# Dense rows of a graph network: four layer products made from x one by one, or from one input by folded weights

## The chip, the core and the metric

The kernel runs on one core of a Trainium2 chip. The metric is the device time of one execution in microseconds. Three runs took 3486.61, 3483.99 and 3440.52 us; the median is 3483.99.

## The reference, cut to what matters

There are 50,000 rows of 128 floats and 12,500 edges sorted by their target. Everything is f32.

```
h = relu(layernorm(x))
x = x + leaky(  (h + neighbours(h)) @ W0.T + b0, 0.01 )
h = relu(layernorm(x))
for l in range(4):                    # GAT layer, with a self loop for each row
    h = h @ W[l]
    h = segment_sum(h[src] * softmax_over_edges_of_dst(...), dst) + b[l]
    h = (h - mean(h)) * rsqrt(var(h) + 1e-5) * gamma[l] + beta[l]
x = x + h
```

A row that is no edge's target has only its self loop, whose softmax weight is 1. For such a row a layer is a product with W[l], a bias, and a normalisation. The kernel computes all 50,000 rows as if they were like that (the dense rows) and writes them out; the rows with edges are computed apart, and their results overwrite the others at the end.

## The kernel before, in words

The weights are centred once in setup (`WC`, L364), so that a product with them has mean zero over its 128 outputs and only the sum of squares is left to find for a normalisation. Gamma and beta of layer l are applied while the turned rows of layer l + 1 are copied out of PSUM (L697).

`dense` (L568) works on groups of 500 rows, four tiles of 125 rows. It is called five times. The first call has `SHARES[0] * DS` = 40 groups and runs beside the 350 gathers and scatters that GpSimd issues for the edges (`first_moves`, L976). The other four calls have 15 groups each, one call before each attention layer, and run beside 100 gathers of edge rows (`refresh`, L1196). All work of a call is one block: every engine meets the others at its end (L615).

A group makes five visits, `k` = 0 to 4, in each of which its rows are normalised (into `Y`), turned by four transposes (L210), copied to `XT` with a relu or with gamma and beta (L695, L697), and multiplied by four products of 128 columns (L221) after a bias product (L217). Visit 0 is the convolution with `W0`, visits 1 to 4 are the layers. In visits 1 to 3 ScalarE squares 512 elements per partition (L680), VectorE sums them (L735), ScalarE takes the root (L202), VectorE inverts it (L759) and multiplies the product by it (L777). After visit 4 the squares are summed by ScalarE itself (L676), and VectorE multiplies by gamma (L787) and adds to the row (`finish`, L795). GpSimd adds beta of the last layer to the row beforehand (L628).

Visits are ordered in rounds (`in_rounds`, L556): five groups make visit 0, then the same five visit 1, and so on. Each engine walks through the visits in its own written order, with fixed offsets between its steps, and waits on semaphores. Rows lie in a ring of ten groups; SP stores a finished group (L159, L160), and loads another into its place one group later. GpSimd spreads its gathers over the whole list of visits.

Around it: `setup` (L277 to L415), the edge terms (L484 to L551), the two convolution stages for the edges (L1003 to L1193), and `attention` (L1210), which uses `XT`, `Y` and all eight banks in a way of its own. The last attention stage ends with 100 scatters into the output (L232).

In setup VectorE makes its steps one after the other: centring, attention vectors, bias rows split into three bf16 parts (L378 to L382), then the masks of the edges. SP waits for the bias parts (L294), stores them as rows of `BR` (L296), fills a table in memory, and then loads the edge attributes.

## Time and profile before

| | us |
|---|---|
| median of three runs | 3483.99 |
| the profiled execution | 3488.22 |
| its span, first to last instruction | 3486.5 |
| the five dense stages | 1693.5 |
| TensorE busy | 2234.9 |
| VectorE busy | 2147.7 |
| ScalarE busy | 1723.3 |
| GpSimd busy | 1377.2 |
| mean granted TensorE clock, share of 2.4 GHz | 0.677 |

A matmul's busy time is that of overlapping instructions taken together, and its mean is that of one instruction from start to end, so the mean times the count is more than the busy time. A product of four tiles shows as eight matmuls, since one f32 tile takes two passes; a transpose shows as one. Engines: PE is TensorE, PEld its weight loads, DVE VectorE, ACT ScalarE, POOL GpSimd, SP the engine that only issues transfers.

### The profile page before, as it was taken

The numbers are of one execution on the slowest core, as the hardware profiler recorded it, in microseconds if no ns is written. First come the engines' busy times: TensorE is split into PE (matmuls) and PEld (weight loads), VectorE is DVE, ScalarE is ACT, GpSimd is POOL, SyncE is SP. The second block draws the span as 40 slices with busy tenths as digits, with TensorE's granted clock in tenths as the row PEclk, the third lists the DMA queues.
The fourth block names the chain that finished last, engine by engine and source line by source line (L and its number), as shares of the span: only waits on it lengthen the run. The fifth ranks groups of instructions, "written<-read, shape, count | busy, mean of one in ns | idle before, by whom it ended". The sixth has DMA issues, their size and how long they took to land. (4 is left out here: it accounts for less than half of the span.)

```text
span 3486.5 us, 45031 instructions
## 1 busy us (share of the span) xinstructions
PE 2234.9 (64%) x11717; PEld 1789.5 (51%) x11717; DVE 2147.7 (62%) x8249; ACT 1723.3 (49%) x5173; POOL 1377.2 (40%) x1089
## 2 busy tenths in 40 slices
PE   2788888886546488890288891188894088797000
PEld 2666666664334366780166781166683066686000
DVE  2367776666888567448767448777446867412880
ACT  0265665554557556444566444566445456422340
POOL 5588778670112466000366000266100076200367
PEclk9976775565555566995567895566697566678555
DMA  6221222110002311000311000311000311003011
GB/s 123 59 50 32 45 67 55 31 19 15 0 0 79 102 34 26 16 1 0 107 34 26 16 1 0 106 34 26 17 1 1 96 26 42 18 1 71 3 31 37
DMA packets 101670, 126.29 MB, mean 36 GB/s; under 512 B 59443, under 2 KB 67563, under 8 KB 98091
## 3 DMA queue, kind: packets, MB, share of 16 engines
q1 hardware_dynamic: 38634, 97.42, 9.8%
q0 software_dynamic: 62400, 25.68, 4.4%
q8 instruction: 90, 1.47, 0.2%
q14 instruction: 114, 0.93, 0.1%
q10 hardware_dynamic: 432, 0.79, 0.1%
HBM read 78.68 MB, written 64.50 MB: 41 GB/s over the span
## 5 line engine op out<-in xcount | busy, mean ns | idle before, releaser
L227 POOL DMA_INDIRECT S<-row_t,INFG x400 | 516.5, 1291 | 1101.1 <-issue 1101.1
L221 PE MATMUL bank<-WC,XT 128*125 128x128 f32 x4800 | 845.9, 330 | 0.0
L221 PEld LDWEIGHTS bank<-WC,XT 128*125 128x125 f32 x4800 | 712.6, 227 | 172.7 <-issue 172.7
L210 PE MATMUL bank<-ident,Y 125*128 125x125 f32 x2200 | 443.7, 354 | 434.1 <-ACT Y L708 396.3
L210 PEld LDWEIGHTS bank<-ident,Y 125*128 125x128 f32 x2200 | 355.0, 189 | 481.1 <-issue 394.1
L217 PE MATMUL bank<-BR,ones 3*125 3x512 bf16 x725 | 385.1, 531 | 125.9 <-ACT XT L697 75.7
L735 DVE TENSOR_REDUCE ss<-Y 125x4 f32<-125x512 f32 x300 | 205.6, 685 | 367.6 <-ACT Y L680 367.6
L221 PE MATMUL bank<-W,XT 128*125 128x128 f32 x1200 | 310.4, 438 | 44.2 <-ACT XT L1033 44.2
L697 ACT ACTIVATE XT<-bank,BC,GC 128x500 f32<-128x500 f32 x300 | 230.3, 768 | 185.7 <-PE bank L210 185.7
L221 PEld LDWEIGHTS bank<-W,XT 128*125 128x125 f32 x1200 | 265.8, 326 | 108.5 <-issue 54.6
L217 PEld LDWEIGHTS bank<-BR,ones 3*125 3x125 bf16 x725 | 107.1, 148 | 273.8 <-ACT XT L697 118.9
L1256 ACT ACTIVATE XT<-bank,BC,GC 128x500 f32<-128x500 f32 x150 | 114.5, 763 | 268.4 <-PE bank L210 268.2
L1282 DVE COPY SCS<-bank 125x8 f32 (+1 forms) x100 | 16.7, 167 | 357.5 <-PE bank L1236 357.5
L695 ACT ACTIVATE XT<-bank 128x500 f32<-128x500 f32 x200 | 116.8, 584 | 225.5 <-PE bank L210 225.5
L680 ACT ACTIVATE Y<-bank 125x512 f32<-125x512 f32 x300 | 177.5, 592 | 95.1 <-PE bank L221 95.1
L777 DVE TENSOR_TENSOR Y<-bank,rr 125x512 f32<-125x512 f32 x300 | 207.5, 692 | 10.2
L708 ACT ACTIVATE Y<-R,nm,rr 125x128 f32<-125x128 f32 x500 | 211.7, 482 | 0.0
L868 DVE SCALAR_TENSOR_TENSOR R<-R,keep (+1 forms) x496 | 189.9, 414 | 34.9 <-ACT R L1373 30.0
L1236 PE MATMUL bank<-SD,XT 128*125 128x64 f32 x1600 | 205.4, 286 | 0.0
L722 DVE BATCH_NORM_STATS2 st<-R 125x6 f32<-125x128 f32 x800 | 173.3, 279 | 49.4 <-issue 49.4
L1236 PEld LDWEIGHTS bank<-SD,XT 128*125 128x125 f32 x1600 | 202.7, 206 | 0.0
L628 POOL TENSOR_TENSOR R<-R,B 125x512 f32<-125x512 f32 x100 | 131.1, 1311 | 164.8 <-PE bank L210 163.3
(205 smaller groups left out, 3961.8 us busy)
## 6 DMA issues: line engine op xcount, KB each, us to landing
R<-in_x SPq DMA_DIRECT2D x100, 224.0 KB
out_rows<-R SPq DMA_DIRECT2D x100, 224.0 KB
row_t<-T SPq DMA_DIRECT2D x20, 1120.0 KB
S<-row_t,INFG POOLq DMA_INDIRECT x400
R<-in_edge_attr SPq DMA_DIRECT2D x1, 5600.0 KB
x_t<-R SPq DMA_DIRECT2D x5, 1120.0 KB
S<-x_t SPq DMA_DIRECT2D x1, 5600.0 KB
R<-in_x SPq DMA_DIRECT2D x100, 26.0 KB
```

The costliest lines, as they stand in the source:

```text
L210: ins = nc.tensor.transpose(ps[:, a * P:(a + 1) * P], t, ident[0:P, 0:P])
L217: nc.tensor.matmul(pz[0:P, :, :], ones3[:, 0:P], BR[:, bias:bias + 1, :].broadcast_to([3, Q, D]), start=True, stop=False, skip_group_check ...
L221: ins = nc.tensor.matmul(pz[0:P, a, :], xt[:, a * P:(a + 1) * P], w, start=bias is None and a == 0, stop=True, skip_group_check=True)
L227: pool.indirect_dma_start(to, None, table, bass.IndirectOffsetOnAxis(ap=idx, axis=0), bounds_check=rows - 1, oob_is_err=False).then_inc(do ...
L680: nc.scalar.activation(Y[:, s, :, :], DPZ[s][0:P, :, :], ACT.Square, scale=D ** -0.5).then_inc(sq_ready.s, 1)
L697: ins = nc.scalar.activation(XT[:, q % 4, :], DPT[q % 3][:, 0:Q * P], ACT.Identity, bias=BC[:, k - 2:k - 1], scale=GC[:, k - 2:k - 1])
L708: ins = nc.scalar.activation(Y[:, s, a, :], rows(g)[:, a, :], ACT.Identity, bias=nm[:, s, a:a + 1], scale=rr[:, s, a:a + 1])
L722: ins = nc.vector.bn_stats(st[:, q % 2, a, :], rows(g)[:, a, :])
L735: nc.vector.tensor_reduce(ss[:, s, :], Y[:, s, :, :], AX.X, ALU.add).then_inc(var_ready.s, 1)
L777: nc.vector.tensor_tensor(Y[:, s, :, :], DPZ[s][0:P, :, :], wide(rr[:, s, :]), ALU.mult).then_inc(y_ready.s, 1)
L868: return nc.vector.scalar_tensor_tensor(column(R, n, a, 1), column(R, n, a, 0), scalar_of(keep, n, a), column(R, n, a, 1), ALU.mult, ALU.add)
L1236: ins = nc.tensor.matmul(PT[r][0:P, a * D:a * D + SW], XT[:, r, a * P:(a + 1) * P], SD[:, l, :], start=True, stop=True, skip_group_check=True)
```

## The change

Setup multiplies the layers' weights: `AC[:, l]` takes the input of the first layer straight to the output of layer l, for l = 0 to 3, without its normalisations. A normalisation divides a whole row by one number, so the product of the folded weights is right up to that number and up to the biases, which enter with factors that depend on the norms before. `PC` and `KC` hold the products of weights and biases that the norms need. `EB` holds the folded bias rows, one block per tile, placed by 16 transfers of one row each.

A group now makes two normalisations (visit 0 and 1 of before), one convolution, and then, from one turned input: four products with six columns (`DOTS`), four products with 384 columns (`layers`, the first three layers side by side), whose squares ScalarE sums one tile and layer at a time (`norms`), sixteen operations on 125x4 on VectorE with three roots on ScalarE that give the factors of the biases (`sums` to `fourth`), one small transpose of these factors (`turn_s`), four products with 128 columns for the last layer, and one f32 bias product over 13 rows and 512 columns. Then it ends as before: squares, root, gamma, addition.

The order is no longer in rounds: in slot t each engine runs a fixed list of steps, each for the group t minus its lag, with lags up to 7. `SHARES` counts groups, 68 in the first call and 8 in each of the others. GpSimd issues `moves * (t + 1) // groups` gathers by slot t, that is all of them within as many slots as there are groups. Rows lie in a ring of 12. The edge stages take their semaphores from a shared set, which changes no instruction order in them. The diff is cut to its core; further small steps (`statistics`, `aggregate`, `invert`, `scale`, `normalise`, `slope`, `leak`, `join`) do what they did.

```diff
-STEPS = 2 + L - 1
+XS = 12
+KS = 3 * Q + 1
...
-SHARES = [8, 3, 3, 3, 3]
+SHARES = [68, 8, 8, 8, 8]
...
-        DPT, DPZ = banks[0:3], [tiles_of(b) for b in banks[3:8]]
+        HALVES = (0, 1, 1, 0)
+        TURN, CONV, LAYERS, LAST = banks[0], tiles_of(banks[1]), banks[2:4], banks[4:6]
+        DOTS = [b[:, 0:Q * 6].rearrange("p (a n) -> p a n", a=Q) for b in banks[6:8]]
+        TURNS = [b[0:KS, 0:P] for b in LAST]
...
+                sp.wait_ge(s_e4, 1)
+                sp.wait_ge(s_ebz, 1)
+                for a in range(Q):
+                    for j in range(3):
+                        sp.dma_start(EB[j * Q + a:j * Q + a + 1, a * D:(a + 1) * D],
+                                     E4[j + 1:j + 2, :]).then_inc(s_eb, 16)
+                    sp.dma_start(EB[KS - 1:KS, a * D:(a + 1) * D], E4[0:1, :]).then_inc(s_eb, 16)
+                sp.wait_ge(s_eb, 16 * 4 * Q)
...
+                pe.wait_ge(s_cent, 1)
+                for l in range(L):
+                    ins = nc.tensor.matmul(PT[1][:, l:l + 1], brow[:, l, :], ones[0:1, 0:1], start=True, stop=l == 0)
+                    if l:
+                        ins = nc.tensor.matmul(PT[1][:, l:l + 1], WC[:, l, :], BC[:, l - 1:l], start=False, stop=True)
+                ins.then_inc(s_ccol, 1)
+                nc.tensor.transpose(PT[2][:, 0:D], WC[:, 0, :], ident[:, :]).then_inc(s_made, 1)
+                for l in range(1, L):
+                    pe.wait_ge(s_kept, l)
+                    nc.tensor.matmul(PT[2 + l % 2][:, 0:D + l], AC[:, l, :], XE[:, l - 1, 0:D + l], start=True,
+                                     stop=True).then_inc(s_made, 1)
+                pe.wait_ge(s_kept, L)
+                for l in range(1, L):
+                    nc.tensor.transpose(PT[2][:, l * D:(l + 1) * D], XE[:, l, 0:D], ident[:, :])
+                for l in range(1, L):
+                    nc.tensor.matmul(PT[3][:, (0, 1, 3)[l - 1]:(0, 1, 3)[l - 1] + l], XE[:, l - 1, 0:D],
+                                     XE[:, l - 1, D:D + l], start=True, stop=True)
+                nc.tensor.transpose(PT[3][0:L, 128:128 + D], XE[:, L - 1, D:D + L], ident[:, :])
+                pe.wait_ge(s_pairs, 1)
+                nc.tensor.matmul(PT[3][:, 16:26], ones[:, :], GP, start=True, stop=True).then_inc(s_made, 1)
...
+                for l in range(1, L):
+                    ch.add(nc.vector.tensor_scalar(AC[:, l, :], WC[:, l, :], GC[:, l - 1:l], None, ALU.mult))
+                dve.wait_ge(s_ccol, 1)
+                ch.link(nc.vector.tensor_copy(CCOL[:, :], PT[1][:, 0:L]))
+                for l in range(L):
+                    dve.wait_ge(s_made, l + 1)
+                    nc.vector.tensor_copy(XE[:, l, D + l:D + l + 1], CCOL[:, l:l + 1])
+                    nc.vector.tensor_copy(XE[:, l, 0:D + l], PT[2 + l % 2][:, 0:D + l]).then_inc(s_kept, 1)
+                dve.wait_ge(s_kept, L)
...
-                    for q in slots:
-                        upto = moves * max(q, 0) // (max(slots) - 8)
-                        upto = min(upto, moves)
+                    for t in slots:
+                        upto = moves * min(t + 1, groups) // groups
                         move(pool, done, upto)
                         done = upto
-                        if q - 8 in visit and visit[q - 8][1] == 1:
-                            pool.wait_ge(*t_done.at(nth[q - 8]))
-                            xs = rows(visit[q - 8][0])
-                            nc.gpsimd.tensor_tensor(xs, xs, B3[:, :].unsqueeze(1).broadcast_to([P, Q, D]),
+                        if 0 <= t - 3 < groups:
+                            pool.wait_ge(*turned2.at(t - 2))
+                            nc.gpsimd.tensor_tensor(rows(t - 3), rows(t - 3),
+                                                    B3[:, :].unsqueeze(1).broadcast_to([P, Q, D]),
                                                     ALU.add).then_inc(beta_added.s, 1)
...
+                    def turn1(g):
+                        pe.wait_ge(*y1_vector.at(g + 1))
+                        pe.wait_ge(*y1_scalar.at(g + 1))
+                        if g - 2 >= 0:
+                            pe.wait_ge(*copied2.at(min(g - 1, groups)))
+                        transposes(TURN, [Y[:, g % 2, a, :] for a in range(Q)]).then_inc(turned1.s, 1)
...
+                    def turn2(g):
+                        pe.wait_ge(*y2_vector.at(g + 1))
+                        pe.wait_ge(*y2_scalar.at(g + 1))
+                        if g + 1 >= 0:
+                            pe.wait_ge(*copied1.at(min(g + 2, groups)))
+                        transposes(TURN, [Y[:, 2 + g % 2, a, :] for a in range(Q)]).then_inc(turned2.s, 1)
...
+                    def last_layer(g):
+                        pe.wait_ge(*s_copied.at(g + 1))
+                        for a in range(Q):
+                            nc.tensor.matmul(last_of(g)[:, a, :], h0(g, a), AC[:, 3, :], start=a == 0, stop=False,
+                                             skip_group_check=True)
+
+                    def add_biases(g):
+                        nc.tensor.matmul(LAST[g % 2][0:P, :], SB[:, g % 2, :], EB[:, :], start=False,
+                                         stop=True, skip_group_check=True).then_inc(last_done.s, 1)
+
+                    def turn_s(g):
+                        pe.wait_ge(*s3_ready.at(g + 1))
+                        if g >= 2:
+                            pe.wait_ge(*multiplied.at(g - 1))
+                        nc.tensor.transpose(TURNS[g % 2], SV[:, g % NS, :],
+                                            ident[0:P, 0:P]).then_inc(s_turned.s, 1)
+
+                    def layers(a):
+                        def op(g):
+                            if a == 0:
+                                pe.wait_ge(*copied2.at(g + 1))
+                                if g >= 2:
+                                    pe.wait_ge(*mixed2.at(g - 1))
+                                for b in range(Q):
+                                    nc.tensor.matmul(DOTS[g % 2][0:P, b, :], h0(g, b), PC[:, :], start=True,
+                                                     stop=True, skip_group_check=True)
+                            if a == 0 and g or a >= 2:
+                                pe.wait_ge(*normed.at(g * Q + (0, 0, 2, 2)[a]))
+                            nc.tensor.matmul(LAYERS[HALVES[a]][0:P, 0:3 * D], h0(g, a), AC[:, 0:3, :], start=True,
+                                             stop=True).then_inc(layers_done.s, 1)
+                        return op
+
+                    for t in slots:
+                        run(t, [(5, last_layer), (3, layers(3)), (2, turn2), (5, add_biases), (0, turn1),
+                                (2, layers(0)), (2, layers(1)), (0, conv), (4, turn_s), (2, layers(2))])
...
+                    def norms(a):
+                        def op(g):
+                            n = g * Q + a
+                            act.wait_ge(*layers_done.at(n + 1))
+                            if a == 0 and g >= NS:
+                                act.wait_ge(*third_sum.at(g - NS + 1))
+                            for l in range(3):
+                                ins = nc.scalar.activation(JUNK[:, HALVES[a] * 3 + l, :], LAYERS[HALVES[a]][0:P, l * D:(l + 1) * D],
+                                                           ACT.Square, scale=D ** -0.5,
+                                                           accum_out=NRM[:, g % NS, l, a:a + 1])
+                            ins.then_inc(normed.s, 1)
+                        return op
...
+                    def s_root(n, ready, done):
+                        def op(g):
+                            act.wait_ge(*ready.at(g + 1))
+                            nc.scalar.activation(SV[:, g % NS, n * Q:(n + 1) * Q], chain(g)[:, n, :], ACT.Sqrt,
+                                                 bias=KC[0:P, (0, 1, 4)[n]:(0, 1, 4)[n] + 1]).then_inc(done.s, 1)
+                        return op
...
+                    for t in slots:
+                        run(t, [(3, copy2), (6, square_last), (0, root1), (1, copy1), (2, root2),
+                                (5, s_root(2, third_sum, s3_ready)), (6, root_last),
+                                (4, s_root(0, first_sum, s1_ready)), (3, norms(0)), (3, norms(1)), (2, normalise2),
+                                (5, copy_s), (4, s_root(1, second_sum, s2_ready)), (1, slope), (0, normalise1),
+                                (3, norms(2)), (3, norms(3))])
...
+                    def sums(g):
+                        c = chain(g)
+                        dve.wait_ge(*normed.at((g + 1) * Q))
+                        nc.vector.tensor_tensor(c[:, 0, :], NRM[:, g % NS, 0, :], dots(g, 0),
+                                                ALU.add).then_inc(first_sum.s, 1)
+                        nc.vector.tensor_tensor(c[:, 3, :], NRM[:, g % NS, 1, :], dots(g, 1), ALU.add)
+                        nc.vector.tensor_tensor(c[:, 4, :], NRM[:, g % NS, 2, :], dots(g, 3), ALU.add).then_inc(mixed1.s, 1)
+
+                    def with_s1(g):
+                        c = chain(g)
+                        dve.wait_ge(*s1_ready.at(g + 1))
+                        for o, k, n in ((5, 3, 2), (6, 7, 4), (7, 8, 5)):
+                            ins = nc.vector.scalar_tensor_tensor(c[:, o, :], s_of(g, 0), k_of(k), dots(g, n),
+                                                                 ALU.mult, ALU.add)
+                        ins.then_inc(mixed2.s, 1)
...
+                    def finish(g):
+                        dve.wait_ge(*multiplied.at(g + 1))
+                        dve.wait_ge(*beta_added.at(g + 1))
+                        nc.vector.tensor_tensor(rows(g), rows(g), FR[:, g % 2, :, :], ALU.add).then_inc(out_ready.s, 1)
+
+                    for t in slots:
+                        run(t, [(3, normalise2), (0, statistics1), (2, leak), (5, with_s2), (2, join),
+                                (0, aggregate1), (2, statistics2), (5, times_s2), (2, aggregate2), (4, sums),
+                                (5, third), (6, sum_last), (7, multiply), (0, invert1), (6, invert_last),
+                                (2, invert2), (0, scale1), (5, fourth), (4, with_s1), (2, scale2), (4, times_s1),
+                                (0, normalise1), (4, second), (7, finish)])
...
-            dense(done * DS, SHARES[l + 1] * DS, C, refresh, [(s_refresh, 16 * C * (l + 1))])
+            dense(done, SHARES[l + 1], C, refresh, [(s_refresh, 16 * C * (l + 1))])
```

## Rows read from the trace of the kernel before

**Rows 1.** The page: the span, and the granted clock in 40 equal slices, in tenths.
```profile
span 3486.5 us, 45031 instructions
PEclk9976775565555566995567895566697566678555
```
**Rows 2.** Busy time in windows, dense stages: first, second, sum of all five.
```profile
core 0: us, PE busy (x) PEld busy (x) DVE busy (x) ACT busy (x) POOL busy (x), PEclk, DMA share, GB/s
138.80:826.20 687.40, 574.83 (x2600) 441.66 (x2600) 455.51 (x1760) 386.86 (x1120) 495.76 (x390) 0.67 0.20 46
1179.50:1432.90 253.40, 198.00 (x975) 151.50 (x975) 171.50 (x660) 145.09 (x420) 148.95 (x115) 0.69 0.15 37
...
sum 1693.50, PE 1357.02 PEld 1041.24 DVE 1142.40 ACT 967.75 POOL 1091.62; mean PE 271.40 PEld 208.25 DVE 228.48 ACT 193.55 POOL 218.32
```
**Rows 3.** The same view: a round, a slow round, parts of a round, 100 us of attention.
```profile
301.90:380.40 78.50, 65.04 (x324) 50.01 (x324) 56.78 (x217) 47.37 (x139) 62.77 (x52) 0.70 0.19 35
556.40:652.00 95.60, 87.96 (x326) 67.96 (x326) 57.87 (x222) 48.84 (x143) 72.34 (x57) 0.50 0.19 38
302.00:349.00 47.00, 38.19 (x144) 29.29 (x144) 34.75 (x147) 24.82 (x74) 39.46 (x32) 0.50 0.26 57
350.00:380.00 30.00, 25.77 (x178) 20.20 (x177) 21.53 (x68) 21.05 (x65) 22.22 (x20) 1.00 0.08 2
2000.00:2100.00 100.00, 100.00 (x785) 88.43 (x784) 43.69 (x111) 50.30 (x93) 0.00 (x0) 1.00 0.00 1
```
**Rows 4.** Groups by line in the round 301.9 to 380.4 us (busy us, mean ns).
```profile
L697 ACT ACTIVATE XT<-bank,BC,GC 128x500 f32<-128x500 f32 x15 | 11.5, 766 | 8.5 <-PE bank L210 8.5
L777 DVE TENSOR_TENSOR Y<-bank,rr 125x512 f32<-125x512 f32 x15 | 10.4, 692 | 0.5
L735 DVE TENSOR_REDUCE ss<-Y 125x4 f32<-125x512 f32 x15 | 10.3, 686 | 16.4 <-ACT Y L680 16.4
L708 ACT ACTIVATE Y<-R,nm,rr 125x128 f32<-125x128 f32 x24 | 10.2, 482 | 0.0
L680 ACT ACTIVATE Y<-bank 125x512 f32<-125x512 f32 x15 | 8.9, 591 | 4.2 <-PE bank L221 4.2
L759 DVE RECIPROCAL rr<-rt 125x4 f32<-125x4 f32 x24 | 4.0, 168 | 0.1
```
**Rows 5.** Timeline (start, length in us), instructions of one line merged.
```profile
301.99 0.26 ACT L676 ACTIVATE Y<-bank 125x128 f32<-125x128 f32 x1
302.24 0.26 ACT L676 ACTIVATE Y<-bank 125x128 f32<-125x128 f32 x1
307.50 2.07 PE L221 MATMUL bank<-W,XT 128*125 128x128 f32 x8
311.98 1.04 PE L210 MATMUL bank<-ident,Y 125*128 125x125 f32 x4
...
508.22 1.14 PE L221 MATMUL bank<-WC,XT 128*125 128x128 f32 x8
```
**Rows 6.** Timeline: one gather, and the pause before it.
```profile
507.61 1.27 POOL L227 DMA_INDIRECT T<-in_x,dstI  x1 [0.30 <-issue]
```
**Rows 7.** Groups by line on GpSimd, 1180 to 1400 us.
```profile
L227 POOL DMA_INDIRECT S<-row_t,INFG x100 | 129.1, 1291 | 51.1 <-issue 51.1
```
**Rows 8.** Single lines, whole span: min/median/max ns; last, busy us and mean.
```profile
L221 PE MATMUL bank<-WC,XT x4800: 272/273/577, 171.4 to 3197.5; 128*125 128x128 f32 x192
L1236 PE MATMUL bank<-SD,XT x1600: 219/273/417, 1441.7 to 3199.2; 128*125 128x64 f32 x178
L764 DVE SCALAR_TENSOR_TENSOR nm<-mv,rr x200: 149/161/1379, 144.4 to 2976.2; 125x4 f32<-125x4 f32 x100
...
L535 PE MATMUL bank<-VE,XT 128*125 128x4 f32 x200 | 42.3, 336 | 0.0
```
**Rows 9.** Timeline in setup: the last bias part, the three transfers after it.
```profile
25.81 0.48 DVE L382 CAST R<-R 1x640 bf16<-1x640 f32 x1
26.32 1.88 SPq L296 DMA_DIRECT2D BR<-R  x3
```
**Rows 10.** Groups by line on TensorE, 2000 to 2100 us: one of two such rows.
```profile
L210 PE MATMUL bank<-ident,S 125*128 125x125 f32 x76 | 11.2, 269 | 0.0
```

625 lines of the change are left out of this document (351 added, 274 removed).

## The prediction

> **What bounds the kernel now.** Read the page first for the span and for the granted clock of TensorE, which swings between its two levels (1.2 and 2.4 GHz) all through the dense stages [rows 1]. Then cut the span into stages: five dense stages, the first with 40 groups of 500 rows and four with 15 each, take 1693.5 of 3486.5 us, 16.9 us a group; that is all that the change rewrites [rows 2]. Then cut one dense stage into rounds of five groups. A round takes 78.5 us, 15.7 us a group, while VectorE is busy 56.8 of it (11.4 a group), ScalarE 47.4 (9.5) and TensorE 65.0 (13.0). Its first 47 us run at clock 0.50 and the next 30 at 1.00, and one round that never got the high clock took 95.6 us [rows 3]. So the half-clock stretches set the pace, with TensorE as the engine that is late and VectorE next behind. The rows of the two clocks differ by almost two: a product of four tiles is 2.07 or 1.14 us [rows 5]. Every dense stage is a block of its own and all engines meet at its end, so it counts with its whole length.
>
> GpSimd matters in a second way. It issues a gather every 1.57 us [rows 6], and each of the four later dense stages has 100 of them [rows 7]: 157 us below which no such stage can go. Now the stages are 251 to 253 us, so the gathers are covered.
>
> **The change, per group.** VectorE: the three wide reductions and the three wide products by the inverse root go, with three inversions [rows 4]: 3 x (0.686 + 0.692 + 0.168) = 4.64 us. Sixteen operations on 125x4 come instead, the recurrence for the three norms. The same form takes 0.161 in the middle [rows 8], so 2.6 us; the bounds are 0.1 (four small ones overlapped) and 0.24 each, 1.6 to 3.8 us. One more normalising tile comes, taken from ScalarE, 0.3 as I estimate. Busy: 11.4 - 4.6 + 2.6 + 0.3 = 9.7 us, and some 30 pauses of 0.03 between operations make 10.6. That is the floor of a slot.
>
> ScalarE: three wide squares and three scaled copies go, 3 x (0.591 + 0.766) = 4.07, and one normalising tile, 10.2 / 24 = 0.43 [rows 4]; three roots go and three come. Twelve squares of one tile with a sum come. Such squares start 0.25 us apart [rows 5], and for the last read of each batch I add half of that: 12 x 0.25 + 4 x 0.13 = 3.5, and a small copy, 0.3 as for one square. So 9.5 - 4.5 + 3.8 = 8.8, with pauses 9.4 us.
>
> TensorE: one tile's product is two passes, a transpose one. From 2.07 us for eight passes, of which the last takes about 0.42, a pass is 0.236 at the low clock, and from 1.14 and 0.27 it is 0.124 at the high one; a transpose is 0.21 by its 1.04 us for four, and half at the high clock [rows 5]. Transposes fall from 20 to 9. Product columns stay the same: conv and last layer are 8 passes each, and the layers' product is 8 passes of 384 columns. A pass of 64 columns lasts 0.219 where one of 128 lasts 0.272 at best [rows 8], so 128 columns more cost 0.107 at the high clock and 0.213 at the low: 0.34 or 0.66 a pass, 2.7 or 5.3 us (bounds: no dearer than a 128 pass, 1.9 at the low clock; three times it, 5.7). The dots with six columns are 8 passes; the nearest, with four, take 42.3 / 200 = 0.21 each where the weights are as large [rows 8], hardly less than 128 columns do, so 0.95 or 1.9. The bias product in f32 has 512 columns twice: 0.9 or 1.8. One bf16 bias remains, 0.2 or 0.43. Sum: high 1.0 + 2.0 + 2.7 + 0.95 + 0.9 + 0.2 = 7.8 us, low 1.9 + 3.8 + 5.3 + 1.9 + 1.8 + 0.4 = 15.1, plus ten pauses of 0.1: 8.8 and 16.1.
>
> **The slot.** I laid the three written orders beside each other with these durations at the high clock. The single bank for turned rows forces turn 2, its copy, turn 1, its copy; the other tight place is that VectorE's last inversion needs ScalarE's root of the same slot. Both fit into about 10.8 us. TensorE then waits three times in a slot: some 1.3 us before turn 1, 1.0 before the third layer tile and 0.8 before the last layer. The long, thin stretch bias, pause, turn 1, dots is like the first visits of a round, where the clock falls now [rows 3], so I expect it to fall in about half of the slots. At the low clock the tiles that follow are long dense passes, as in the stretches before which it rises, so it should soon return. The slack hides part; I charge 0.8 us a slot. **11.6 us** is my slot.
>
> **The first stage** has 68 groups in 76 slots: 61 full ones, seven that fill, at the low clock and by their latencies 80 us, and eight that drain, 45: 61 x 11.6 + 125 = 833 us, where 687.4 stood [rows 2]. GpSimd has 350 gathers and 68 additions, 418 x 1.57 = 656, and stays hidden.
>
> **The four others** have 8 groups in 16 slots, 131 us by TensorE's low-clock sum up to the twelfth slot. But all 100 gathers stand in the first eight steps of GpSimd's queue, 12.5 a step, and group g's addition of beta stands behind step g + 3. The fifth comes after 100 gathers and five additions: 105 x 1.57 = 165 us. VectorE's finish waits for it, and behind that wait stand its operations for the later groups. Then come three drained slots, 3.5, 9.5 and 1 us, and the store, 3 us: 182 us where 252 stood. This term hardly depends on the clock. Its bounds: 165 + 10 and 165 + 25 us.
>
> **Setup.** The new chain of TensorE and VectorE (four small products, copies, transposes, pairs) delays the bias split, which ends at 26.3 now, by about 16 us; SP then issues 16 one-row transfers at 0.63 each, by the three like them, 1.88 us [rows 9], and waits 2 us more. Edge attributes are behind them on SP, and the first gathers and the next block behind the barrier: + 27 us on the path, bounds 12 and 38.
>
> **The sum** against the profiled execution's own 3488.2 us: - 1693.5 + 833 + 4 x 182 + 27 = - 105.5, so 3383 us. The runs' median is 3484.0, 4 us below it, their lowest 3440.5; I say 3383, 2.9% under the median. A difference below 2% I take as what a measurement of this kernel can't tell from none, since its runs lie 1.3% apart.
>
> **Rivals.** (a) The clock stays high. For it: the round's dense half has 1.00 [rows 3]. Then a slot is 10.8: 61 x 10.8 + 125 = 784, and the time 3334 us. The Trainium skill (TensorE: Matmul & The Clock Gate, Part 4: PE-mode transpose) says that transposes do not count as activity for the clock; by that rule 11 transposes fewer out of 20 would favour this rival. A hundred microseconds of attention hold clock 1.00 with twice 76 transposes among 785 matmuls [rows 3, 10], which neither bears it out nor refutes it. Chance 0.17.
>
> (b) The handoffs cost more than laid out: three engines in fixed order, each within 25% of the slot, and many small dependent steps on two of them. Now a slot is 15.7 with the busiest of the two at 11.4, a ratio of 1.38; at 1.25 over 10.6 it is 13.2, the first stage 930 us, the time 3480 us, no change. It is also the case in which the folding buys nothing, as what left the wide operations comes back in narrow ones. Chance 0.22.
>
> (c) Slower: the clock stays low. Its place is TensorE in the full slots of the first stage, its price 16.1 us and waits, say 16.3: 61 x 16.3 + 125 = 1119 us, the time 3669 us. It decides from a slot of 14.4 us on, where the time is 2% over. For it: TensorE would be busy only 8.8 of 11.6 us, 76%, with waits in between, and a whole round did run at 0.50. Against it: in such a slot its passes stand close behind each other, three times as long as now, and attention, packed like that, got and kept the high clock. The same page (Why this matters for your kernels) says that idle gaps between bursts of matmuls put the clock back to half; by that rule the pauses above would bring this about, and the trace agrees as far as the clock is 0.50 in the 47 us in which TensorE is busy 38.2 and waits for normalised rows [rows 3]. Chance 0.12.
>
> **The numbers.** My forecast, with slots of 11.1 to 12.5 us, has 0.45, and 3350 to 3438 us; (a) 0.17, (b) 0.22, (c) 0.12; 0.04 is for something in setup or code that I don't see. Faster by over 2% (below 3414) takes three quarters of the forecast, all of (a) and a little of (b): 0.34 + 0.17 + 0.05 = 0.56. Within 2%: the rest of the forecast and of (b), 0.28. Slower: (c) and the last 0.04, 0.16. The range of 8 in 10 goes from 3320, just under (a), to 3510, beyond (b).
>
> **What would show it.** The first stage at 833 us, its stores 11.6 us apart; VectorE busy about 9.7 and ScalarE 8.8 us a group; TensorE's granted clock in it between 0.7 and 0.9. A 384-column pass at 0.34 or 0.66 us. Four stages of 182 us with GpSimd's gathers 1.57 us apart without gaps, and VectorE waiting for the addition of beta before its finish. The block after setup begins 27 us later. The forecast is wrong if stores lie over 12.5 us apart, or if the later stages take more than 190 us.

## The result, and the profile after

The changed kernel takes 3225.4 us (median of 4 runs, 3220.5 to 3230.3) where the kernel before, beside it on the same chip, takes 3483.5: a ratio of 0.929, 95% interval 0.921 to 0.936. That is 158 us under the forecast of 3383 and 95 us under the range. The profiled execution took 3226.0 us. Its page:

```profile
span 3224.0 us, 44576 instructions
...
PEclk9999988899655557569656589556598556697555
...
L1016 DVE TENSOR_TENSOR R<-R 125x512 f32<-125x512 f32 x100 | 81.9, 819 | 327.8 <-POOL R L687 327.6
```

The clock is now high for most of the first dense stage (granted 0.90, where the stage before had 0.67 [rows 2]). Windows of the changed kernel: the first dense stage, two of the four others, and two stretches from the middle of the first: 250 us of it, and 61 us in which the clock never fell.

```profile
160.00:861.10 701.10, 632.56 (x2992) 401.87 (x2992) 647.71 (x3468) 584.67 (x3128) 542.91 (x418) 0.90 0.27 66
1213.50:1403.90 190.40, 96.13 (x352) 59.86 (x352) 71.96 (x408) 71.68 (x368) 140.38 (x108) 0.63 0.13 31
...
2606.80:2797.40 190.60, 98.70 (x352) 61.81 (x352) 72.34 (x408) 71.89 (x368) 140.55 (x108) 0.62 0.13 30
350.00:600.00 250.00, 233.49 (x1139) 149.35 (x1137) 241.47 (x1316) 220.59 (x1184) 205.12 (x158) 0.90 0.31 77
...
350.00:411.00 61.00, 54.97 (x301) 35.42 (x299) 61.00 (x341) 57.20 (x311) 50.71 (x40) 1.00 0.28 61
```

The five dense stages take 701 + 4 x 190.5 = 1463 us instead of 1693.5 [rows 2], 230 less. In the middle window a group takes 9.7 us (in the full slots of the first stage stores are 8.8 to 11.8 us apart, 583 us for 60 of them), against 15.7 in a round before [rows 3], and VectorE is busy 97% of the time, without a pause where the clock is high (61.00 of 61.00 us). GpSimd is fuller than its 205 us busy say. Its groups by line in those 250 us, and VectorE's last operation of a group, which needs the addition of beta:

```profile
L241 POOL DMA_INDIRECT T<-in_x,dstI x86 | 114.4, 1330 | 30.5 <-issue 30.5
L246 POOL DMA_INDIRECT info_t<-INFO,repI x47 | 59.2, 1260 | 14.1 <-issue 14.1
L687 POOL TENSOR_TENSOR R<-R,B 125x512 f32<-125x512 f32 x25 | 31.9, 1278 | 0.7
...
L1016 DVE TENSOR_TENSOR R<-R 125x512 f32<-125x512 f32 x26 | 17.6, 678 | 0.0
```

Before the addition of beta (L687) it waits 0.7 us in all; every other pause is its own issue. 205.1 + 44.6 + 0.7 is the whole window: GpSimd is always either issuing or adding. A gather with its pause takes 1.64 us on average here (218.2 us for 133 of them), so a group gives it 5.15 x 1.64 + 1.28 = 9.7 us, as much as the slot. Yet nobody waits for it in this window: L1016 has no idle time before it, and in the whole first stage each group's addition is done 25 to 34 us before VectorE needs it. GpSimd issues its last gather of the stage 655 us after the stage began and then waits for the last groups to be turned.

The rest of the 258 us: setup is 22 us longer (the block behind it begins at 55.5 instead of 33.2 us), and the four attention blocks that project messages and scores, whose code did not change, take 144.5, 140.0, 140.7 and 140.4 us instead of 140.2, 149.4, 158.9 and 167.8, 51 less in all. The first rows are the beginning of the last such block before, the other two that of the changed kernel:

```profile
3032.00:3101.00 69.00, 68.97 (x284) 60.17 (x285) 5.89 (x18) 13.02 (x20) 0.00 (x0) 0.50 0.00 1
...
3101.00:3140.00 39.00, 39.00 (x307) 34.50 (x307) 6.95 (x21) 14.54 (x23) 0.00 (x0) 1.00 0.00 1
```
```profile
2797.60:2808.00 10.40, 10.35 (x43) 8.88 (x44) 0.00 (x0) 3.45 (x5) 0.00 (x0) 0.50 0.01 2
2808.00:2850.00 42.00, 42.00 (x326) 36.86 (x326) 7.87 (x24) 13.40 (x21) 0.00 (x0) 1.00 0.00 1
```

TensorE is equally full in both, but the clock stays at its lower level for 69 us in the one and 10 in the other. In time order the low beginnings were 9, 28, 49 and 69 us before, 18, 8, 10 and 10 after.

### The profile page after: what moved, and what is told of

The parts are those of the page before. It is cut to its first block and busy times, and to the rows that moved or that the text cites. A ratio compares the mean times of both kernels' runs of the same rounds, so it can differ in the third digit from the quotient of the medians.

```text
span 3224.0 us, 44576 instructions
## 1 busy us (share of the span) xinstructions
PE 1867.9 (58%) x9650; PEld 1361.5 (42%) x9650; DVE 1945.6 (60%) x8980; ACT 1628.2 (51%) x6973; POOL 1390.2 (43%) x1089
## 5 line engine op out<-in xcount | busy, mean ns | idle before, releaser
L224 PE MATMUL bank<-ident,Y 125*128 125x125 f32 x1000 | 193.0, 327 | 439.3 <-ACT Y L774 234.6
L759 PE MATMUL bank<-AC,XT 128*125 128x384 f32 x800 | 396.5, 609 | 17.8 <-ACT R L822 17.7
L224 PEld LDWEIGHTS bank<-ident,Y 125*128 125x128 f32 x1000 | 141.4, 170 | 559.2 <-DVE Y L913 228.1
L822 ACT ACTIVATE R<-bank 125x128 f32<-125x128 f32 x1200 | 311.6, 274 | 101.5 <-PE bank L759 100.8
L1016 DVE TENSOR_TENSOR R<-R 125x512 f32<-125x512 f32 x100 | 81.9, 819 | 327.8 <-POOL R L687 327.6
L822 ACT ACTIVATION_READ_ACCUMULATOR R<-bank 125x1 f32 x1200 | 246.9, 206 | 0.0
L235 PE MATMUL bank<-WC,XT 128*125 128x128 f32 x1600 | 237.0, 293 | 0.0
L1492 ACT ACTIVATE XT<-bank,BC,GC 128x500 f32<-128x500 f32 x150 | 114.3, 762 | 216.7 <-PE bank L224 216.4
L235 PEld LDWEIGHTS bank<-WC,XT 128*125 128x125 f32 x1600 | 197.8, 194 | 47.5 <-issue 47.5
L1090 DVE SCALAR_TENSOR_TENSOR R<-R,keep (+1 forms) x496 | 189.5, 412 | 33.2 <-ACT R L1609 29.1
L231 PE MATMUL bank<-BR,ones 3*125 3x512 bf16 x325 | 158.3, 487 | 54.9 <-ACT XT L1377 48.0
L759 PEld LDWEIGHTS bank<-AC,XT 128*125 128x125 f32 x800 | 155.3, 226 | 76.5 <-ACT R L822 30.6
L734 PEld LDWEIGHTS bank<-AC,XT 128*125 128x125 f32 x800 | 124.0, 230 | 67.3 <-ACT SB L839 57.7
```

Of the source, the lines that this page charges most:

```text
L224: ins = nc.tensor.transpose(ps[:, a * P:(a + 1) * P], t, ident[0:P, 0:P])
L231: nc.tensor.matmul(pz[0:P, :, :], ones3[:, 0:P], BR[:, bias:bias + 1, :].broadcast_to([3, Q, D]), start=True, stop=False, skip_group_check ...
L235: ins = nc.tensor.matmul(pz[0:P, a, :], xt[:, a * P:(a + 1) * P], w, start=bias is None and a == 0, stop=True, skip_group_check=True)
L734: nc.tensor.matmul(last_of(g)[:, a, :], h0(g, a), AC[:, 3, :], start=a == 0, stop=False, skip_group_check=True)
L759: nc.tensor.matmul(LAYERS[HALVES[a]][0:P, 0:3 * D], h0(g, a), AC[:, 0:3, :], start=True, stop=True).then_inc(layers_done.s, 1)
L822: ins = nc.scalar.activation(JUNK[:, HALVES[a] * 3 + l, :], LAYERS[HALVES[a]][0:P, l * D:(l + 1) * D], ACT.Square, scale=D ** -0.5, accum_ ...
```

## The experiments

Those low beginnings differ between executions of one kernel (e9), so kernels are compared below by the lengths of their dense stages in the profiled execution; medians stand beside them. The changed kernel's own first stage took 701 us in one execution and 708 in another (e9), so 7 us there are no difference. Where a stage ends with gathers (e1, e4, e10, e12), its length is given up to the end of the gathers, and attention's first instruction follows some 2 us later; in the changed kernel, where a later stage ends with stores, it follows at once.

**e1, the split of groups alone, in the old kernel.**

```
-SHARES = [8, 3, 3, 3, 3]
+SHARES = [12, 2, 2, 2, 2]
```

> The kernel before, with 60 groups in the first dense stage and 10 in each of the four others (12, 2, 2, 2, 2 rounds instead of 8, 3, 3, 3, 3). Theory A (the split is no gain of its own; the shorter slot is): 12 rounds in the first stage at the 80 us they take now, 687 + 4 x 80 = 1007 us; each later stage loses a round of 78 us, 251 - 78 = 173 us; five stages 1700 us, the time 3490 us, within 1%. Rival B (the split is a good part of the gain): later stages at 165 or less and rounds in the long first stage at under 78.5: five stages 1590, the time under 3400 us. Rival C (GpSimd's gathers stand in the way once a stage is short, as in the changed kernel): later stages at 190, the time 3560 us. Attention is the same code; where its clock rises in each of its four blocks is read beside it.

Measured: 1003 us, then 208, 182, 179 and 180: 1752 us, 59 more than before. The median is 3511 us (3471 to 3563) beside 3507 (3451 to 3559). A holds for the time, which is the same within 1%, though the later stages are 6 to 35 us longer than it said: the split is no gain by itself. Attention began low for 18, 9, 10 and 10 us here, with the old dense code, so the 51 us of attention do not come from the folding either.

**e2, the old split in the changed kernel.**

```
-SHARES = [68, 8, 8, 8, 8]
+SHARES = [40, 15, 15, 15, 15]
```

> The changed kernel with the old split of 40, 15, 15, 15 and 15 groups. Theory A (GpSimd's queue is the wall of short stages: 850 gathers and 100 additions of beta in all five stages together, 1.57 us each, so the split hardly matters): first stage 390 x 1.57 = 612 us and its end, 640; each other one 115 x 1.57 = 181 us and its end, 200; five stages 1440 us against 1463 measured for 68, 8, 8, 8, 8; the time 3205 us, within 1% of the changed kernel. Rival B (the split carries the gain: each later stage pays a fill and a drain over 15 groups, 8 x 9.65 + 189 = 257 us): five stages 640 + 1028, the time 3430 us.

Measured: 645 us and 201, 201, 201 and 202.5: 1450 us. A holds to 10 us: what the first stage lacks in groups it loses to GpSimd's queue, with stores 15.8 us apart. The median is 3256 us (3210 to 3308). The profiled execution took 3262; one of its attention blocks began with 120 us at the low clock and is 51 us longer than the others, without which it would be near A's 3205.

**e3, the written order undone.** Same operations and lags, each engine's slot ordered from the oldest group to the newest, as far as waits across engines allow. VectorE's list, shortened:

```
-run(t, [(3, normalise2), (0, statistics1), (2, leak), (5, with_s2), (2, join),
-        (0, aggregate1), (2, statistics2), (5, times_s2), (2, aggregate2), ...
+run(t, [(7, multiply), (7, finish), (6, sum_last), (6, invert_last),
+        (5, with_s2), (5, times_s2), (5, third), (5, fourth), (4, sums), ...
```

> The changed kernel with the same operations and the same lags, but each engine's order within a slot written group by group, oldest first (as far as the waits across engines allow), instead of interleaved. Theory A (the interleaved order is what fills VectorE to 97%): chains such as sum, root, inverse of one group stand behind each other with a wait for the other engine in each, some 8 round trips of 0.4 to 1.5 us, slot 13 us or more: first stage 930 us or more, the time 3450 us or more. Rival B (lags of seven slots already give every engine enough to do, the order inside matters little): slot under 10.5 us, first stage under 760, the time under 3290 us.

Measured: 4277 us, the first stage 1645 us, stores 24 us apart. A holds, and my price for it was far too small. A window of 240 us (ten groups), and VectorE's inversions in it:

```profile
800.00:1040.00 240.00, 140.11 (x446) 85.06 (x446) 94.06 (x510) 96.74 (x470) 80.41 (x64) 0.62 0.14 36
```
```profile
L889 DVE RECIPROCAL rr<-rt 125x4 f32<-125x4 f32 x30 | 5.3, 178 | 128.7 <-ACT rt L789 76.8 <-ACT rt L794 49.2 <-ACT rt L850 2.7
```

All engines are at 60% or less. VectorE waits 128.7 us for ScalarE's roots: statistics, root and inverse of one group now stand in a row, while the root sits at the end of ScalarE's slot. With this order the folded arithmetic gives a kernel 22% slower than the one before (4277 to 3507 us).

**e4, beta on VectorE in the four later stages.**

```
 @block.gpsimd ...
-    if 0 <= t - 3 < groups:
+    if first_group == 0 and 0 <= t - 3 < groups:
 @block.vector ...
+    def add_beta(g):                          # run as (5, add_beta)
+        if first_group:
+            dve.wait_ge(*turned2.at(g + 1))
+            nc.vector.tensor_tensor(rows(g), rows(g), B3[...], ALU.add).then_inc(beta_added.s, 1)
```

> The changed kernel; in the four later dense stages the addition of beta goes from GpSimd, where it stands behind the gathers, to VectorE (one 125x512 addition a group, 0.7 us). Theory A (each later stage ends with GpSimd's queue and what hangs on its last additions): the fifth addition no longer comes after 105 x 1.57 us; the stage is bounded by its 100 gathers, 157 us and their landing, 160 to 168 us where 190.5 stand; the time 3225 - 4 x 26 = 3120 us. Rival B (fill and drain over 16 slots set the length, GpSimd only covers it): 190 stays to within 5 us, the time 3215 us or more.

Measured, one such stage:

```profile
1218.90:1386.50 167.60, 86.80 (x352) 55.11 (x352) 73.80 (x416) 71.26 (x368) 130.20 (x100) 0.65 0.15 35
```

167.6, 167.4, 168.5 and 166.7 us: A holds. What is left is the 100 gathers, 158 us, and their landing. The profiled execution took 3218 us, only 8 less than that of the changed kernel, since two of its attention blocks began with 110 and 69 us at the low clock: some 80 us were won in the dense stages (the first took 706) and some 70 of them lost there. The median is 3206.6 (3180 to 3218).

**e5 to e7, less work on one engine each,** executed once each, as e8 was.

```
 e5: - tensor_tensor(SL[:, g % 2, :, :], SL[:, g % 2, :, :], CONV[0:P, :, :], ALU.max)
     + tensor_tensor(SL[:, g % 2, 0:1, :], SL[:, g % 2, 0:1, :], CONV[0:P, 0:1, :], ALU.max)
       (the residual's addition likewise)
 e6: - activation(JUNK[..., :], LAYERS[...][0:P, l * D:(l + 1) * D], ACT.Square, ...)
     + activation(JUNK[..., 0:16], LAYERS[...][0:P, l * D:l * D + 16], ACT.Square, ...)
 e7: - matmul(LAYERS[...][0:P, 0:3 * D], h0(g, a), AC[:, 0:3, :], ...)
     + matmul(LAYERS[...][0:P, 0:n * D], h0(g, a), AC[:, 0:n, :], ...)    # n = 3 if g < 1 else 1
       (and the six-column products only for g < 2)
```

> The changed kernel; VectorE's maximum of the leaky step and its addition of the residual work on one row tile of four (three tiles of these two operations are left out, about 0.95 us of VectorE a group). Theory A (VectorE is the bound of the first stage, 9.3 of 9.65 us busy): stores 0.6 to 0.95 us closer, the first stage 701 - 61 x 0.7 = 658 us. Rival B (the slot is set by handoffs between engines or by TensorE, busy 9.0): the first stage within 10 us of 701. The later stages stay at 190 in both, as GpSimd's queue ends them.

> The changed kernel; ScalarE's twelve squares a group for the three folded norms read 16 of 128 columns (the rest is left out), each about 0.07 us shorter, 0.9 us of ScalarE a group. Theory A (VectorE is the bound): the first stage within 10 us of 701. Rival B (ScalarE or the ring TensorE - ScalarE of layer tiles and norms is the bound): 0.5 us or more a slot, the first stage 670 or less.

> The changed kernel; TensorE's product for the three norms has 128 columns instead of 384 and the six-column products are left out (from the second or third group on), together 2.9 us a group at the high clock out of 9.0. Theory A (TensorE is not the bound, and it stays at its high clock or the slack covers the low one): the first stage within 10 us of 701. Rival B (a TensorE with less to do falls to the low clock, and then its 6.1 us become some 11): slots of 11 us, the first stage 780 us. Rival C (TensorE is the bound): slots under 9.2, the first stage under 675.

Measured: first stages of 695, 685 and 694 us, later ones 189 to 191. The middle window of each, in that order:

```profile
350.00:600.00 250.00, 238.98 (x1134) 152.19 (x1133) 229.46 (x1322) 220.46 (x1190) 205.50 (x160) 0.88 0.31 77
```
```profile
350.00:600.00 250.00, 230.19 (x1154) 148.92 (x1155) 244.70 (x1332) 197.94 (x1202) 204.07 (x158) 0.94 0.31 77
```
```profile
350.00:600.00 250.00, 216.24 (x929) 156.59 (x929) 243.30 (x1326) 221.54 (x1192) 205.00 (x161) 0.71 0.31 77
```

Relieving ScalarE brings 16 us; the 6 and 7 us of VectorE and TensorE are no more than two executions of one kernel differ. GpSimd's column stands at 204 to 205.5 in all of them. So my theory A of e5, by which less work on VectorE brings 43 us, fell. e6 came in between its two cases. In e7 TensorE, with about a third of its work gone, was granted 0.71 instead of 0.90, and the stage was not longer.

Two things in the traces say why so little came. GpSimd finished its last gather of the stage at 816, 812, 817 and 811 us in the changed kernel and in e5 to e7: its queue has a length of its own, 650 to 655 us, and the last groups need some 30 us behind it. That makes a floor of about 685 us, an estimate from these traces, and e6 reaches it: its additions come 9 to 15 us before VectorE needs them in the last third of the stage, and GpSimd waits 2 us in all before them, where it waits 13 in the changed kernel. And in e5 VectorE was held up for longer, as told under e8: 46 us in the middle window instead of 38.5.

**e8, a first stage with and without gathers in one run.**

```
 upto = moves * min(t + 1, groups) // groups
+if first_group == 0:
+    upto = moves * min(t + 1, 36) // 36
```

> The changed kernel, with all 350 gathers and scatters of the first stage in GpSimd's first 36 steps, 9.7 a step, and none after that. So one run shows slots with and without gathers. Theory A (VectorE's small operations are held up beside GpSimd, L900 has 145 ns at the least and 1705 at the most): in the slots after the gathers no VectorE operation is lengthened by more than 0.3 us, VectorE's busy time falls from 9.3 to about 8.3 us a group and stores come 8.6 to 9.2 us apart. Rival B (the long ones come from elsewhere, or GpSimd costs nothing): 9.65 us apart in the gatherless slots too. In the first 36 slots GpSimd sets the pace in both, 9.7 x 1.57 + 1.3 = 16.5 us.

Measured: the first stage took 924 us, the execution 3454. Stores are 17.0 us apart with 9.7 gathers a slot (A: 16.5). In the slots without they are 8.9 apart on average, as A said: 8.2 to 8.3 in most and 11.5 in every fifth. A window among those, and one such period:

```profile
900.00:1000.00 100.00, 97.77 (x499) 63.73 (x498) 92.21 (x580) 94.67 (x525) 14.14 (x11) 0.93 0.20 58
...
888.80:895.60 6.80, 6.80 (x21) 4.29 (x20) 5.16 (x28) 5.03 (x26) 0.00 (x0) 0.50 0.25 77
895.60:933.10 37.50, 36.50 (x202) 23.98 (x202) 35.35 (x229) 36.61 (x206) 6.41 (x5) 1.00 0.19 56
```

The slot of 11.5 us is the one in which the clock is low, for 6.8 us. Busy per group (11.4 groups in the 100 us, by the counts of instructions): TensorE 8.6, ScalarE 8.3, VectorE 8.1 us. The last is 1.2 less than the 9.3 of the changed kernel beside gathers, for the same operations. The lengthened VectorE operations are all but gone: together they had 38.5 us too much in the middle window of the changed kernel, 1.5 us a group, and 0.9 us in eleven groups here, in two operations of 0.63 us, 0.2 us longer than A allowed. Where they come from is seen in the changed kernel's timeline (start, length), and in the durations of three lines in the middle window (min/median/max ns; L954 has one of its inputs in PSUM):

```profile
549.38 0.47 DVE L954 SCALAR_TENSOR_TENSOR CH<-SV,KC,bank 125x4 f32<-125x4 f32 x3
...
549.68 1.27 POOL L241 DMA_INDIRECT T<-in_x,dstI  x1 [0.30 <-issue]
...
549.88 2.40 DVE L962 SCALAR_TENSOR_TENSOR CH<-CH,KC,SV 125x4 f32<-125x4 f32 x2
...
550.98 1.27 POOL L687 TENSOR_TENSOR R<-R,B 125x512 f32<-125x512 f32 x1
...
552.21 0.59 DVE L913 TENSOR_SCALAR Y<-R,rr,nm 125x128 f32<-125x128 f32 x2
```
```profile
L954 DVE SCALAR_TENSOR_TENSOR CH<-SV,KC,bank x77: 202/205/213, 349.8 to 590.2; 125x4 f32<-125x4 f32 x77
...
L962 DVE SCALAR_TENSOR_TENSOR CH<-CH,KC,SV x52: 210/221/2262, 350.2 to 592.5; 125x4 f32<-125x4 f32 x52
...
L900 DVE SCALAR_TENSOR_TENSOR nm<-mv,rr x25: 142/1130/2105, 357.7 to 589.8; 125x4 f32<-125x4 f32 x25
```

An operation on 125x4 elements that takes 0.21 us takes 2.26 and ends with GpSimd's addition, at 552.3; until then nothing else runs on VectorE. Twenty-six operations are lengthened so in the 26 slots, all of them with both tensors in SBUF (13 of L900, 6 of L982, 3 of L1000, 2 each of L962 and L976), for 35.7 of the 38.5 us; each ends 0.03 us after an addition. The other 2.8 us are eight operations of L913, up to 0.75 us long with no addition beside them, as 13 are in e10. One tensor in SBUF can be enough: L913 and L922 have one and a factor and an offset per row, none was held up by an addition in the changed kernel's first stage, but 8 were in e6, 5 in e5 and 2 in e7, up to 2.4 us instead of 0.35. In e8 GpSimd makes the same additions, but each as soon as TensorE has turned its group, and 9 of 11 meet no such operation: what counts is when in VectorE's slot the addition comes, and that is what the gathers ahead of it in the queue shift. The Trainium skill (SBUF — State Buffer, Who interferes with whom) says that a VectorE operation with two SBUF inputs and a GpSimd one that reads SBUF cannot run together, and that the later one is held up until the other is done. The rows of the changed kernel agree on which lines are struck and on where they end. They begin up to 1 us before the addition's own record, and L913 and L922 in e5 to e7 are struck with one SBUF tensor; this part of the rule leaves both open.

**e9, the changed kernel again**, on the chip of e10 to e12.

> The changed kernel as it is, beside the next three. Theory A (the first part of each attention block runs at the low clock for a time that is drawn anew in each run): dense stages within 5 us of 701, 190, 190, 190, 190, but the low-clock beginnings of the four attention blocks differ from the 18, 8, 10 and 10 us of the profiled run of the result, and the time with them, by up to 60 us a block. Rival B (they belong to the kernel's own timing): 18, 8, 10 and 10 again.

Measured: 708 us and 190, 190, 190, 191; the low beginnings 9, 10, 38 and 8 us. A holds. The four runs lay at 3224, 3234, 3243 and 3316 us (median 3238.7, ratio to before 0.935, 0.927 to 0.943).

**e10, beta on VectorE everywhere**: e4 without its conditions on first_group, and no addition on GpSimd.

> The changed kernel, with the addition of beta on VectorE in all five dense stages. Theory A (in the first stage GpSimd is nearly the bound, 5.15 gathers x 1.58 + 1.28 = 9.4 us a slot, and its addition also holds up one VectorE operation in each slot, 1.5 us): VectorE 9.3 - 1.5 + 0.7 = 8.5 us busy a slot, GpSimd 8.1, TensorE 8.4 to 9.0; stores 8.8 to 9.0 us apart; first stage 650 to 660 us, the others 168. Dense stages 1325 us where 1463 stand. Rival B (VectorE's own work is the bound and the long operations are not GpSimd's doing): 9.3 + 0.7 = 10 us a slot, first stage 722 us.

Measured: 655 us, then 167, 167, 168 and 167, in all 1323 us, as A's sum said, and stores 9.0 us apart. The middle window, and the line of L900 in it:

```profile
350.00:600.00 250.00, 241.82 (x1216) 156.41 (x1216) 236.34 (x1427) 232.26 (x1266) 196.12 (x147) 0.92 0.32 83
```
```profile
L900 DVE SCALAR_TENSOR_TENSOR nm<-mv,rr 125x4 f32<-125x4 f32 x28 | 4.4, 157 | 0.0
```

27.5 groups instead of 26, VectorE busy 8.6 us each (A: 8.5) although it does one wide addition more, and L900 at 0.157 us instead of 0.824 on average. The experiment takes two things away at once, 1.28 us a group from GpSimd's queue and the holding up of VectorE. No run separates them; that VectorE never waited for an addition in the changed kernel's first stage speaks for the second. The median was 3165 us (3140 to 3193); one attention block of the profiled run began low:

```profile
1337.20:1456.90 119.70, 119.64 (x493) 104.84 (x494) 25.90 (x66) 26.86 (x57) 0.00 (x0) 0.50 0.00 1
```

**e11, products on the idle TensorE ahead of attention.**

```
+if first_group:
+    pe.wait_ge(*normed.at(groups * Q))
+    pe.wait_ge(*almost.at(1))          # GpSimd, ahead of its last step
+    for i in range(18):
+        nc.tensor.matmul(LAYERS[i % 2][0:P, :], h0(0, 0), AC[:, :, :], start=True, stop=True)
```

> The kernel of e10, with eighteen products of 512 columns, whose result nobody reads, on the idle TensorE in the last 20 us of each of the four later dense stages, until the attention block begins. Theory A (attention begins at the low clock because TensorE was idle, and what it does then, with its transposes, can leave the clock low for 8 to 120 us): attention begins at the high clock in all four blocks; each is 4 to 5 us shorter than the 141.9 us of a block with a short low beginning, 137, and none is longer, so the times of the runs lie within 0.3%. Rival B (the clock falls at the block's boundary in any case): low-clock beginnings as before. The dense stages as in e10.

Measured: it failed as built. The products did raise the clock, but they ended early, TensorE was then idle for 6 us, and the clock fell 2 to 3 us before each block and stayed low for 10, 102, 113 and 10 us: the blocks took 141.6, 184.5, 189.3 and 141.4 us; median 3148 us (3134 to 3179). The first of them, TensorE's timeline:

```profile
1311.67 18.02 PE L775 MATMUL bank<-AC,XT 128*125 128x512 f32 x36 [39.27 <-POOL spare L687]
1335.79 1.07 PE L225 MATMUL bank<-ident,S 125*128 125x125 f32 x4 [6.09 <-PEq L680]
```

**e12, all of it with a new split.**

```
-SHARES = [68, 8, 8, 8, 8]          -XSRC_EARLY = C // 2
+SHARES = [56, 11, 11, 11, 11]      +XSRC_EARLY = 62
```

> The kernel of e11, with 56 groups in the first dense stage and 11 in each other one, and 62 instead of 50 of the first gathers in the edge block ahead, where GpSimd is idle at the end. Sum by the bounds found: first stage 48 slots x 8.9 + 112 = 540 us, against 338 gathers x 1.58 = 534 us on GpSimd; later stages still 100 x 1.58 and the end, 168 us each; the edge block stays 104. Five dense stages 1215 us, 110 fewer than in e10. Rival: a later stage with 11 groups needs 112 + 3 to 4 slots of 8.9, which stays under 168; if fill and drain are longer than that, 185 us each and only 40 us gained.

Measured: 3008 us (3001.5 to 3012.4), ratio to before 0.871 (0.865 to 0.876); the changed kernel beside it had 3239. The first stage took 571 us, 31 more than the sum, the others 169, 169, 168 and 167: 1245 us. Most of the 31 us are GpSimd's: its 338 gathers came 1.68 us apart on average, not 1.58, and the last was issued 23 us after the last store of the stage. In three of its four attention blocks, after idle gaps of 1.4 to 1.9 us, the clock fell 1 to 2 us after the block's first instruction and was low for 7 us only (142, 142 and 141 us), and in the first, after 0.8 us, never (138). The first dense stage's window:

```profile
160.30:731.70 571.40, 499.37 (x2464) 318.91 (x2464) 486.40 (x2912) 476.99 (x2576) 450.43 (x338) 0.90 0.29 68
```

**e13, e12 with 28 products instead of 18.**

> The kernel of e12 with 28 unread products of 512 columns instead of 18 at the end of each later dense stage, so that they last until the attention block begins. In e11 and e12 TensorE had been idle for up to 6 us between the last of them and the block, and the clock had fallen in all blocks but one, where the gap was 0.8 us. Theory A (the gap let it fall): no gap over 1 us, all four attention blocks at the high clock from their first product, 138 us each up to the point where 142 stood (168 in the last one), the time 3000 us and the runs within 0.3% of each other. Rival B (the clock's level at a block's start is chance, the one high beginning too): low-clock beginnings of 8 us or more in most blocks, the time 3008 us or more, some 5 us more where the products outlast the stage.

Measured: all four attention blocks at the high clock from their first product on, and six runs within 3026.4 to 3032.9 us, 0.2%. In the first, the gap ahead is 0.3 us:

```profile
1235.48 25.90 PE L775 MATMUL bank<-AC,XT 128*125 128x512 f32 x56 [15.76 <-POOL spare L687]
1261.68 0.62 PE L225 MATMUL bank<-ident,S 125*128 125x125 f32 x4 [0.30 <-PEq L680]
```

A holds as a mechanism. The gain does not: the 28 hold the block back by 8 us, so that, counted from the end of the gathers, the blocks take 144 us, and the median is 3030, not 3000. From the first load of a later stage to the last product of its attention block e13 takes 313 to 314 us and e12 306 to 310, 22 us more in all four, which is the whole difference of the two medians. (The chips differ, and with them the kernel before; the ratio to it is 0.869, 0.863 to 0.874.) Some 20 to 22 products would be the number to try, an estimate from e12's gaps; it was not tried.

## Why the prediction was wrong in size

**The sum, term by term** (forecast, measured): first stage 833, 701; four later ones 182, 190.5 each; setup + 27, + 22; attention 0, - 51. From 3383 us: - 132 + 34 - 5 - 51 = 3229, where 3226 was measured. Of the first stage's 132 us, 61 x (11.6 - 9.7) = 116 are the slot and 16 the filling and draining (109 us for my 125).

**The step that failed: "some 30 pauses of 0.03 between operations make 10.6. That is the floor of a slot."** There are no such pauses: VectorE is busy 97% of the middle window and 61.00 of 61.00 us while the clock is high. And its small operations overlap: the three of L954 take 0.47 us together (timeline under e8), not 3 x 0.206. Without GpSimd in its way it needs 8.1 us a group (e8), where I had 9.7 and then 10.6. That it was busy 9.3 us in the changed kernel, near my 9.7, is luck: 1.4 of them are holding up, which I did not have. With a floor of 10.6, a slot of 10.8 laid upon it and 0.8 for the clock, I was at 11.6. The slot is 9.7 us, and without gathers 8.9 (e8). ScalarE (8.6 us a group for 8.8), TensorE (9.0 for 8.8) and the 384-column pass (starts 0.32 or 0.64 us apart for 0.34 or 0.66) came as forecast.

**The charge for the clock, 0.8 us a slot, was too high here.** The granted clock of 0.90 was at the top of my 0.7 to 0.9. Between 240 and 800 us of the changed kernel the slots away from low stretches are 9.45 us long in the median and all slots 9.7 on average, so the low clock costs about 0.2 us a slot, while VectorE is held up anyway. Where it is not, the clock costs more: 8.25 and 8.9 us in e8, 8.5 and 9.0 in e10, so 0.5 to 0.7 us a slot, close to my charge. e7, with the clock at 0.71, doesn't show that it is free, because TensorE has less to do there. The Trainium skill's section that rival (c) names (TensorE: Matmul & The Clock Gate, Why this matters for your kernels) is about longer gaps than the 0.8 to 1.3 us that I had laid out, so it gave that rival no support. Rival (a), 3334 us, was nearer than my forecast, and its condition, a clock that is mostly high, came true; its slot of 10.8 did not, since it stands on the same floor.

**"GpSimd has ... 418 x 1.57 = 656, and stays hidden."** The product was right (the last gather was issued 655 us after the stage began), and the conclusion left out what GpSimd does to VectorE. At 9.7 us a slot GpSimd has no pause left, and its additions hold VectorE up for 1.4 us. e8 and e10 show that this costs 0.7 to 0.8 us a slot: 8.9 without gathers, 9.0 without additions, 9.7 with both; 655 instead of 701 us for the stage.

**The later stages** went by the step as written: gathers without gaps, VectorE waiting for the addition of beta (327.6 us in the page's row of L1016), then the drained slots. It came to 190.5, beyond my bound of 190 by a hair: the fifth addition ended 172 us after the stage began, not 165, and the end behind it was 18 us, not 17. e4 took the queue away and left 167.6.

**Setup** (22 for 27 us) was right: the 16 transfers are there, 0.6 us each, from 40.6 us on. **Attention** I had at no change, without looking at how its four blocks differ in the trace of before, though their low beginnings of 9 to 69 us stood in it. Its 51 us are luck and no work of the change: the old dense code has the short beginnings too (e1), and the changed kernel has a long one in e9. Without them the time would be 3277 us, still under the range. Of the other rivals, (b) and (c) needed slots of 13.2 and 16.3 us; nothing of them appeared, although e3 shows how near (b) lies: the same operations in a plainer order take 24 us a slot.

**What is shown and what isn't.** Shown: the split alone gives nothing (e1), nor does the old split harm (e2); the written order is worth 14 us a slot against the plainer one that was tried (e3); GpSimd's queue sets the length of the later stages (e4); in the first its additions lengthen VectorE's operations (e8, e10), and taking them away brings 46 us (e10). Not shown: how these 46 us divide between the holding up and the shorter queue, and how the gain divides between folding and order, since the old operations were not tried in the new order. And why a full TensorE stays at the low clock for 8 us in one block and 120 in the next is open: it follows an idle TensorE (gaps of 6 us in e11: 10 to 113 us low; of 1.4 to 1.9 in e12: 7; of 0.3 in e13: none), but its length differs from run to run of one kernel, and a longer gap does not mean a longer stretch (7.7 us in the changed kernel and e9: 8 to 38 us low; 63 to 67 in e10: 9 to 120).

## What to carry to other kernels

Take an engine's busy time from a window, not from a sum of durations, and add no pauses that no row shows; then compare the new slot with every queue, and above all with the one that the old slot hid with a margin. Where three engines stand within 10% of each other, as in the changed kernel, the order inside the slot can decide more than the arithmetic, and taking work from the busiest one moves the time little until the one behind it is relieved as well. Work moved to an idle GpSimd may still be paid for on VectorE: here 0.7 us on VectorE replaced 1.4 us of being held up.

## What the hardware showed that was not expected

- GpSimd's 125x512 addition held up one VectorE operation on 125x4 elements in nearly each slot, 1.4 us a slot, up to 2.26 us for one of 0.21; all 26 of the middle window have two tensors in SBUF (L900 and L962 among them), none of the 77 with one in PSUM was struck (L954, 213 ns at most). In e5 to e7 it also struck 15 operations on 125x128 with a single tensor, in SBUF (L913, L922, up to 2.4 us). Without gathers between them, the same additions met VectorE twice in eleven groups (e8).
- In e8's slots without gathers the clock fell for 6.8 us in every fifth slot, once after 37.5 us in which TensorE was busy for 36.5, and each time cost 3.2 us (11.5 for 8.25).
- In attention TensorE was busy 119.64 of 119.70 us at 0.50 (e10), and other runs of the same block left that level after 9 to 18 us. The Trainium skill (TensorE: Matmul & The Clock Gate, Part 4: PE-mode transpose) says that transposes do not count as activity; the low stretches contain them, but so do the high ones of the same block, and no run here takes them out, so the rows neither bear it out nor refute it. Each such stretch costs about half its length: the first block of e10 is 51 us longer than its third, for 110 us more at the low clock. It may well be what scatters the times (3440 to 3487 us for the kernel before, 3224 to 3316 in e9, 0.2% in e13, where it is gone), but only one execution of each kernel has a trace, and e3, with low beginnings of 9 us in each block, scatters by 0.2% too.
